# Cross-attention scores for the maxima: the low parts of two heads side by side in the array, and one maximum over two banks

## What is computed

```python
q_big = jnp.einsum('bshk,hkq->bshq', (x @ Wq.T).reshape(b, s, H, K), w_kc_q)      # H = 16 heads
kv_rope = kv_c * cos[None] + _rotate_half(kv_c) * sin[None]                       # 2 x 512 x 64
q_r = jnp.einsum('bshq,hqr->bhsr', q_big, W_qr)
k_r = jnp.einsum('bld,hdr->bhlr', kv_rope, W_kr)
scores = jnp.einsum('bhsr,bhlr->bhsl', q_r, k_r)
attn = jax.nn.softmax(scores, axis=-1)
ctx_c = jnp.einsum('bhsl,bld->bhsd', attn, kv_rope)
```

## Time and profile before

| | us |
|---|---|
| three runs | 259.76, 259.8, 258.25 |
| median | 259.76 |
| profiled execution, own time | 261.29 |
| its span, first to last instruction | 259.6 |

### The profile page before, as it was taken

The page is one execution under the profiler, slowest core; times in us unless marked ns, Lnnn a source line. Parts: engine busy times, 40 slices in busy tenths (PEclk is TensorE's granted clock), DMA queues, the critical chain, the costliest instruction groups (busy, mean ns, idle before and its releaser), DMA issues.

```text
span 259.6 us, 4343 instructions
## 1 busy us (share of the span) xinstructions
PE 240.5 (93%) x1563; PEld 172.7 (67%) x1563; DVE 195.9 (75%) x351; ACT 132.5 (51%) x285; POOL 103.3 (40%) x135
## 2 busy tenths in 40 slices
PE   6989999988997989999899999999999999998991
PEld 4478797754654556776577776678676777767870
DVE  1377577899764699859889999995768895886684
ACT  1545367566368347646576666564455524413350
POOL 7297400000114306646555555564364535001272
PEclk9999999999998699999999999999999999999997
DMA  7999940000000840000000000000000000000002
GB/s 240 326 277 313 413 176 3 1 1 3 0 3 0 153 91 0 3 0 0 4 1 0 0 3 0 0 3 0 3 0 0 1 3 1 0 3 0 1 0 83
DMA packets 4502, 13.67 MB, mean 53 GB/s; under 512 B 513, under 2 KB 1281, under 8 KB 4353
## 3 DMA queue, kind: packets, MB, share of 16 engines
q1 hardware_dynamic: 4048, 11.29, 13.3%
q0 software_dynamic: 432, 2.10, 3.7%
HBM read 14.43 MB, written 0.52 MB: 58 GB/s over the span
## 4 chain that ended last, share of the span: by engine, by line
PE 71%; DVE 15%; DMA 5%; ACT 4%; issue 2%; SPq 2%; POOL 0%; POOLq 0%; ACTq 0%
PE ps L842 11%; PE ps L792 7%; PE ps L819 5%; PE ps L776 5%; PE ps L820 5%; PE ps L793 5%; PE ps L856 5%; DMA wq<-in_wq 5%; PE ps L632 3%; PE ps L921 3%; DVE mneg L1346 3%; PE ps L829 3%; PE ps L694 2%; PE ps L679 2%; PE ps L572 2%
## 5 line engine op out<-in xcount | busy, mean ns | idle before, releaser
L1181 ACT ACTIVATE probs<-ps 128x512 f32<-128x512 f32 x64 | 38.0, 597 | 46.7 <-PE ps L820 45.7
L1408 DVE TENSOR_REDUCE xmneg<-ps 128x1 f32<-128x512 f32 x64 | 43.0, 688 | 16.5 <-PE ps L793 16.1
L445 POOL TENSOR_TENSOR psums<-psums,probs 128x512 f32<-128x512 f32 x30 | 38.6, 1288 | 10.8 <-ACT probs L1181 8.2
L441 POOL TENSOR_TENSOR psums<-probs 128x512 f32<-128x512 f32 x15 | 19.2, 1281 | 43.1 <-ACT probs L1181 43.1
L792 PE MATMUL ps<-KA,QA 128*128 128x512 f32 x64 | 30.8, 481 | 2.7 <-DVE xmneg L1408 1.9
L842 PE MATMUL ps<-probs,kv_dup 128*64 128x256 f32 x256 | 31.2, 385 | 0.0
L1426 DVE RECIPROCAL xrcp<-ps 128x256 f32<-128x256 f32 x16 | 28.0, 1751 | 2.4 <-PE ps L829 2.4
L1173 ACT ACTIVATE QA<-ps 64x256 fp32r<-64x256 f32 x64 | 24.2, 378 | 10.9 <-PE ps L776 9.7
L1346 DVE TENSOR_REDUCE mneg<-ps 128x4 f32<-128x1024 f32 x16 | 19.6, 1224 | 9.5 <-PE ps L572 9.1
L819 PE MATMUL ps<-QA,KA 128*128 128x512 f32 x64 | 26.0, 406 | 0.0
L398 POOL TENSOR_TENSOR rstd<-mv,eps_col 128x1 f32<-128x1 f32 x12 | 2.3, 189 | 59.3 <-DVE mv L1334 59.0
(11 more groups left out here) (162 smaller groups left out, 459.1 us busy)
## 6 DMA issues: line engine op xcount, KB each, us to landing
wu<-in_wu SPq DMA_DIRECT2D x4, 640.0 KB, 8.4
wq<-in_wq SPq DMA_DIRECT2D x4, 512.0 KB, 13.5
wcT<-in_wcT SPq DMA_DIRECT2D x4, 384.0 KB, 12.3
wE<-in_wE SPq DMA_DIRECT2D x4, 320.0 KB, 11.2
w13T<-in_w POOLq DMA_DIRECT2D x1, 1024.0 KB, 8.0
x1T<-in_xT SPq DMA_DIRECT2D x1, 512.0 KB, 3.8
kvp<-in_kv POOLq DMA_DIRECT2D x1, 512.0 KB, 6.2
x_nat<-in_xn SPq DMA_DIRECT2D x1, 512.0 KB, 18.2
```

The source lines that it names most:

```text
L445: g.tensor_tensor(psums[:, s, :], psums[:, s, :], probs[:, s, kc, :], ALU.add).then_inc(xadd_sb, 1)
L1181: a.activation(probs[:, n % 2, kc, :], ps[:, 2 + u % 2, :], ACT.Exp).then_inc(xexp_sb, 1)
L1408: v.tensor_reduce(xmneg[:, n % 4, qt, hh:hh + 1], ps[:, u % 2, :], AX.X, ALU.max, negate=True).then_inc(xmax_sb, 1)
```

## The change

`xmax(n, qt)` is called twice per unit instead of four times. Each call computes query tile qt for both heads: two 128-row matmuls, head 0 into bank 0 and head 1 into bank 1, and then the low parts of both with 64 rows, since the rows of the maxima aren't needed here. Head 0 reads `QB` and `KB` in partitions 0 to 63. Head 1 reads copies on partitions 64 to 127, `QU` (3 buffers) and `KU`, so that its matmul uses the other half of the array; in units 0 and 1 it reads `QB` and `KB` as head 0 does. SP makes the copies by DMA: `KU` once per sequence, `QU` for each unit from 2 on when `query_lo(n)` is done. DVE takes the maxima of both banks with one reduction of 128x1024. PE calls `xmax` in steps r = 0 and r = 2, each time waiting for the reduction before (`xmax_sb`). On DVE the old attention's `attn_norm`, `xrecip`, `xnorm` and, in units 3 and 4, `norm_stats` move ahead of the unit's second reduction. PE waits for the second residual sum before a transpose in unit 14.

```diff
--- before.py
+++ after.py
@@ -178,6 +178,8 @@
         sb("behind_moe", [P, 4416 - 3584], scope=late)
         QA = sb("QA", [P, NQ, 2, SEQ], F32R, scope=late)
         QB = sb("QB", [DC + 4, NQ, 2, SEQ], F32R, scope=late)
+        QU = sb("QU", [P, 3, SEQ], F32R, scope=late)
+        KU = sb("KU", [P, 2 * LK], F32R, scope=late)
         xmneg = sb("xmneg", [P, 4, 2, 2], scope=late)
         xmhi = sb("xmhi", [P, 4, 2, 2], F32R, scope=late)
         xmsplit = sb("xmsplit", [P, 4, 2, 2, 2], scope=late)
@@ -248,6 +250,7 @@
         kvT_ps = sem("kvT_ps")
         kvT_sb = sem("kvT_sb")
         kvT_lo = sem("kvT_lo")
+        kv_up = sem("kv_up")
         xbo = sem("xbo")
         proj_ps = [sem(f"proj_ps{k}") for k in range(2)]
         r_sb = [sem(f"r_sb{k}") for k in range(3)]
@@ -261,6 +264,7 @@
         q_ps = sem("q_ps")
         qhi_sb = sem("qhi_sb")
         qlo_sb = sem("qlo_sb")
+        qup = [sem(f"qup{k}") for k in range(2)]
         qzero = sem("qzero")
         xmax_ps = sem("xmax_ps")
         xmax_sb = sem("xmax_sb")
@@ -324,6 +328,16 @@
                 hs = slice(4 * g, 4 * g + 4)
                 sp.dma_start(wu[:, hs, :], wu_in[:, hs, :]).then_inc(ld_wu[g], 16)
             sp.dma_start(sh[:], sh_in).then_inc(ld_sh, 16)
+
+            for b in range(2):
+                ks = slice(b * LK, (b + 1) * LK)
+                sp.wait_ge(qhi_sb, 4)
+                sp.dma_start(KU[DC:P, ks].bitcast(F32), KA[0:DC, ks].bitcast(F32)).then_inc(kv_up, 16)
+            for n in range(2, NUNIT):
+                sp.wait_ge(qlo_sb, 2 * n + 2)
+                if n >= 5:
+                    sp.wait_ge(xmax_ps, 2 * (n - 3) + 2)
+                sp.dma_start(QU[DC:P, n % 3, :].bitcast(F32), QB[0:DC, n % NQ, 1, :].bitcast(F32)).then_inc(qup[n % 2], 16)
 
             out_rows = out.rearrange("b (u p) d -> p (b u) d", p=P)
             for t in range(NT):
@@ -776,22 +790,30 @@
                     mm = pe.matmul(ps[:, query_bank(n), 0:SEQ], M_sb[:, c, p, :], x1T[:, c, b * SEQ:(b + 1) * SEQ], start=(c == 0), stop=(c == 1))
                 mm.then_inc(q_ps, 1)
 
-            def xmax(n, r):
-                b = n // NPAIR
-                hh, qt = r // 2, r % 2
-                u = 4 * n + r
-                s = n % NQ
-                if r == 0:
+            def xmax(n, qt):
+
+                b, s = n // NPAIR, n % NQ
+                u = 2 * n + qt
+                if qt == 0:
                     pe.wait_ge(qzero, n + 1)
                     pe.wait_ge(qhi_sb, 4 * n + 4)
                     pe.wait_ge(qlo_sb, 2 * n + 2)
-                if u >= 2:
-                    pe.wait_ge(xmax_sb, u - 1)
+                    if n == 2:
+                        pe.wait_ge(kv_up, 32)
+                    if n >= 2:
+                        pe.wait_ge(qup[n % 2], 16 * (n // 2))
+                if u >= 1:
+                    pe.wait_ge(xmax_sb, u)
                 q = slice(qt * P, qt * P + P)
-                o = bank(u % 2)
-                pe.matmul(o, QA[:, s, hh, q], KA[:, b * LK:(b + 1) * LK], start=True, stop=False)
-                pe.matmul(o, QB[:, s, hh, q], KB[:, b * LK:(b + 1) * LK],
-                          start=False, stop=True).then_inc(xmax_ps, 1)
+                ks = slice(b * LK, (b + 1) * LK)
+                for hh in range(2):
+                    pe.matmul(bank(hh), QA[:, s, hh, q], KA[:, ks], start=True, stop=False)
+                pe.matmul(bank(0), QB[0:DC, s, 0, q], KB[0:DC, ks], start=False, stop=True)
+                if n < 2:
+                    mm = pe.matmul(bank(1), QB[0:DC, s, 1, q], KB[0:DC, ks], start=False, stop=True)
+                else:
+                    mm = pe.matmul(bank(1), QU[DC:P, n % 3, q], KU[DC:P, ks], start=False, stop=True)
+                mm.then_inc(xmax_ps, 1)
 
             def xmaxT(n):
 
@@ -851,7 +873,7 @@
                 if t == 1 and p == 0:
                     pe.wait_ge(r_sb[1], 1)
                 if t >= 2 and p == 0:
-                    pe.wait_ge(xmax_sb, 4 * NUNIT)
+                    pe.wait_ge(xmax_sb, 2 * NUNIT)
                     pe.matmul(o, ident[:], x1[:, t, :], start=True, stop=False)
                 mm = pe.matmul(o, ctxn[:, p, t * P:(t + 1) * P], U_sb[:, p, :], start=(p == 0 and t < 2), stop=(p == NPAIR - 1))
                 if p == NPAIR - 1:
@@ -944,8 +966,8 @@
                         attn_exp(NGRP - 1, r // 2)
                     if n < 3 and r == 0:
                         attn_sum(NGRP - 3 + n)
-                    if n < NUNIT:
-                        xmax(n, r)
+                    if n < NUNIT and r % 2 == 0:
+                        xmax(n, r // 2)
                     if LAG <= n < NUNIT + LAG:
                         xexp(n - LAG, r)
 
@@ -970,6 +992,7 @@
                         for p in range(3 * (r - 1), min(3 * r, NPAIR)):
                             out_proj(1, p)
                     if n == NE + 6 and r == 3:
+                        pe.wait_ge(r_sb[1], 2)
                         normed_T(1, x2, 0, 7)
                     if n == NE + 7 and r == 1:
                         pe.wait_ge(nT_sb[1], 1)
@@ -1401,15 +1424,12 @@
                     v.tensor_tensor(QB[0:DC, n % NQ, hh, :], ps[h, query_bank(n), 0:SEQ], QA[h, n % NQ, hh, :].bitcast(F32),
                                     ALU.subtract).then_inc(qlo_sb, 1)
 
-            def xmax(n, r):
-                u = 4 * n + r
-                hh, qt = r // 2, r % 2
-                dve.wait_ge(xmax_ps, u + 1)
-                v.tensor_reduce(xmneg[:, n % 4, qt, hh:hh + 1], ps[:, u % 2, :], AX.X, ALU.max,
-                                negate=True).then_inc(xmax_sb, 1)
+            def xmax(n, qt):
+                dve.wait_ge(xmax_ps, 2 * n + qt + 1)
+                v.tensor_reduce(xmneg[:, n % 4, qt, :], ps[:, 0:2, :], AX.X, ALU.max, negate=True).then_inc(xmax_sb, 1)
 
             def xmax_split(n):
-                dve.wait_ge(xmax_sb, 4 * n + 4)
+                dve.wait_ge(xmax_sb, 2 * n + 2)
                 if n >= 4:
                     dve.wait_ge(xmT_ps, n - 3)
                 v.tensor_copy(xmhi[:, n % 4], xmneg[:, n % 4]).then_inc(xmhi_sb, 1)
@@ -1484,20 +1504,16 @@
                     norm_apply(1, 1, x2)
                 if n in (4, 5):
                     norm_apply(0, n - 2, x1)
-                if n < NUNIT:
-                    xmax(n, 1)
-                if n < NUNIT:
-                    xmax(n, 2)
                 if n < 3:
                     attn_norm(NGRP - 3 + n)
-                if n < NUNIT:
-                    xmax(n, 3)
-                    xmax_split(n)
-                if n in (3, 4):
-                    norm_stats(0, n - 1, ps[:, 7, 0:D], x_nat)
                 if n >= LAG + 2:
                     xrecip(n - LAG - 2)
                     xnorm(n - LAG - 2)
+                if n in (3, 4):
+                    norm_stats(0, n - 1, ps[:, 7, 0:D], x_nat)
+                if n < NUNIT:
+                    xmax(n, 1)
+                    xmax_split(n)
                 if n + 2 < NUNIT:
                     query_lo(n + 2)
                 if NUNIT <= n < NUNIT + 2:
```

## The result

The changed kernel takes 270.13 us (median of 267.62 to 270.92) beside 259.39 us before: ratio 1.0395, 95% interval 1.035 to 1.0439. Run again later beside the kernel before, it took 267.41 us, ratio 1.0304 (1.0243 to 1.0366). It is slower, as forecast (266.9, range 262 to 271). The profiled execution took 267.62 us, 6.3 us more than that of before (261.29).

A forecast was written before the change was run, and what follows sets the result against it. PE was taken to bound the kernel from unit 3 on, with PE, ACT and DVE in turn before unit 2. 2.8 (start) + 4.2 (shape changes) + 1.9 (reduction wait) - 1.8 (given back) = +7.1 on 259.8: 266.9 us, range 262 to 271.

The forecast's parts named there:

- Changes of shape: PE in each xmax call: switching between whole columns and halves costs more than the pair saves, +4.2 us over units 3 to 15.
- The wait on the joint reduction: Second xmax call of units 6 to 11, 14, 15: PE waits for the reduction holding both banks, +1.9 us in all.
- DVE keeps a microsecond: End of a steady unit: DVE finishes about 8 us in, before the next reduction is asked for at 9, so no wait.
- The start: Units 0 to 2: longer reductions and the wait for both banks make unit 3's first call 2.8 us late.
- Given back: Units 5 and 14: PE's waits on DVE of 0.46, 0.97 and 0.41 us go with the new order, -1.8 us.
- The added waits cost nothing: PE's new waits, including the residual sum in unit 14: their events come 3 us or more earlier, cost 0.
- The copies are hidden: SP's DMA copies of QU and KU: they land in about 1.7 us, before they are wanted, cost 0.
- The sum: Whole kernel: 2.8 + 4.2 + 1.9 - 1.8 = +7.1 us, giving 266.9 us, 2.7% slower.
- Rival 2: Near 90 to 100 us: PE's longer standing still brings a second half-clock stretch, +3 us, 270 us; chance 0.10.
- Rival 1: Every xmax call: switching between whole and half columns is free, so the kernel gets faster, -2.5 us, 257.3 us; chance 0.09.
- rival 4: The 64-row pairs in xmax don't run together: +6.6 less 1.9 us of hidden stall, 271.6 us; chance 0.03.
- rival 3: Unit 2: the DMA copies land late, after 9.8 us, +5 us, 272 us; chance 0.05.

The follow-up runs named there:

- a_whole: The changed kernel with the second matmul of both heads whole (no halves, no copies by DMA), one reduction per call kept: 264.86 us, ratio 1.0159 to the kernel before.
- e_serial: The changed kernel, but both heads' 64-row matmuls read QB and KB in partitions 0 to 63, sharing one array half: 273.40 us, ratio 1.0548 to the kernel before.
- h_two2: The changed kernel with two 128x512 reductions per call, PE waiting for each bank by itself, run a second time: 267.33 us, ratio 1.0316 to the kernel before.
- b_late: The changed kernel, but from unit 3 on the second call comes after the third step of the exponentials: 269.25 us, ratio 1.0324 to the kernel before.
- c_order: The kernel before, whole matmuls and four reductions kept, with only the changed kernel's DVE order from unit 3 on: 257.40 us, ratio 0.9866.
- d_warm: The changed kernel with ten float32 filler matmuls of 256 columns on PE in unit 1: 269.76 us, ratio 1.0326 to the kernel before.
- f_early: The changed kernel from unit 3 on, with units 0 to 2 as in the kernel before: 265.07 us, ratio 1.0226 to the kernel before.

## Why the prediction was right, step by step

- *What bounds the kernel*: right for units 3 to 14: PE is the bound there, and what the halves added came out one for one in unit 12. In unit 15 it is DVE's norm step at one place (0.76 us).
- *Changes of shape, 0.20 us each, two in a call against a step of 0.235 saved, +0.165 us a call*: right in mechanism and size. 0.19 us a change, 0.22 us a pair, 0.16 us a call (units 12 of a_whole, e_serial and the changed kernel). The late start alone is 0.09 us (150.32 against 149.89 + 0.235 + 0.1). The Trainium skill, TensorEngine Tiling (Array Packing), Key Properties, has the drain, and these traces agree: there is a late start at each change. The estimate of 0.05 us for it, from the Trainium skill's TensorE: Matmul & The Clock Gate, Part 2, is too little, so the measurement decides.
- *The wait on the joint reduction, 0.24 us in 8 units*: right in mechanism, a little large. Between the second transpose's end (149.10) and the call (149.23) lie 0.13 us, and the exposed weights add 0.1. But the unit shows 0.20: 7.87 less 7.35 less the 0.32 of the two calls. h_two2 gets 0.16 of it back. In unit 15 the wait for the norm step takes its place. What I left out is ACT's wait right behind it, so that no reordering around the call gets this back (b_late).
- *DVE keeps a microsecond*: right. It ends its unit's work with the low part of the next query and waits 0.91 us for the pair.
- *The start, +2.8 us*: right to 0.1 us, 104.17 against 101.33 us, and at its end by the way worked out: at 100.65 the first reduction of unit 2 ends. That it is so close is luck, for in between two errors cancelled: query product 2 ended not 0.95 us late but 0.8 us early (86.91 + 1.07, against 87.10 + 1.72 in the earlier trace rows, as less of unit 0 ran at half clock), and query product 3 ran at half clock.
- *Given back, -1.8 us*: too small, and right only in part. c_order, which has this part alone, is 2.1 us shorter from unit 3 on by its trace: 1.70 in unit 5, where 1.43 was forecast, and 0.37 of DVE's lateness in every second unit, which wasn't. The 0.41 us in unit 14 doesn't come of the order: c_order still has that wait. It is gone in the changed kernel, which has no third reduction to wait for (that unit lasts 7.25 us there, and 7.21 before). And the 0.97 us before 124.64 are just what the norm step took too long (1.38 less 0.41): with a short step they would not have been there, whatever the order.
- *The added waits cost nothing*: right. But the sum has no term for the norm step in unit 15, which the later first reduction holds up; it costs 0.76 us.
- *The copies are hidden*: right, 1.9 us at the median and 4.0 at most, and no wait on `qup` shows in the waits of PE.
- *The sum, +7.1*: the profiles give +6.3 (265.9 against 259.6): 2.8 at the start, 2.5 in units 3 to 14 and 1.1 in unit 15. My terms make 2.8, 3.8 and 0.6. So the sum is closer than its parts, as what was given back and the smaller wait were missed on one side and unit 15 on the other.
- *Rival 2, a second stretch at half clock, +3 us, 0.10*: the one whose chance I had too low. A second stretch came in both profiles of the changed kernel, but with a shorter first one, so that it cost nothing in sum there (0.984 against 0.981 before). The other three executions of the first series had 0.972 or 0.973, and so the first median, 270.1, lies 3 us above my forecast, inside the range only because the range had room for this rival; the second series, at 0.973 to 0.989, has 267.4. That the forecast is within 0.5 us of the second median is luck too, as the clock alone moves it by more. At full clock the changed kernel has 263 us and that of before 257, 6 us, and the rest of the first difference (10.7) is clock. The cause that the rival named, PE standing still, isn't shown: a_whole stands still as long and stays at full clock. *Rival 1* (free changes) is refuted by a_whole, *rival 4* by the common start of the pair, *rival 3* by the landing times.

## What to carry to other kernels

Two small matmuls that run side by side in the array save one step (0.22 us for 512 columns) but each way into and out of that shape costs nearly as much (0.19 us) when the stream around it has another one. So by these numbers a lone pair loses, and several pairs in a row, or a pair where the shape must change anyway, could pay: an estimate, 2 x 0.22 - 2 x 0.19 = 0.06 us for two pairs, and no run here has them. One reduction over two banks takes the double buffer away, which cost PE up to 0.40 us a unit here (a_whole); it can only pay where the reducing engine is the bound, and here PE was. When a reduction gets longer, look also at what stands behind it on its engine: the transpose that waited for the norm step in unit 15 cost 0.76 us, more than a steady unit lost (0.52). Changes that come in a bundle are worth taking apart: the order on DVE alone, without the rest, is 0.85% faster than the kernel before.

## What was not expected of the hardware

The same program ran at mean granted clocks of 0.972 to 0.989, which is 4.5 us of 267, with stretches at 1.2 GHz in different places, three times even in a part that all kernels share (a mean of 0.66 from 57 to 62 us in the profiles of d_warm, e_serial and f_early, and 1.00 in those of both kernels). The profiled execution of before (0.981) was below the usual 0.99 of its kernel and that of after (0.984) above most of its own first series, so the two spans differ by 6.3 us where the medians differ by 10.7. A norm step on DVE of 128x256, 1.38 us in unit 5 of the kernel before, lasts 0.41 us in c_order, and the copy of 128x4 maxima takes 0.17 to 1.13 us. In the trace of the kernel before, the long ones lie beside work on POOL; a run that moves that work alone was not made.
